# Layer 2 attention scores by 32x64 tiles of the array, one head per row group and PSUM bank; a subtraction moved from VectorE to GpSimd; VectorE's order changed

## The reference

```
# x: [128, 64, 384]; adj: [128, 64, 64], passed as both spatial and edge encoding
q = (x @ Wq.T).reshape(b, n, 12, 32); k, v likewise (v + bv)
scores = einsum('bqhd,bkhd->bhqk', q, k) * 384**-0.5 + (adj + adj)
scores = where(any(scores != 0, -1), scores, -inf)
p = nan_to_num(softmax(scores, -1))
out = einsum('bhqk,bkhd->bqhd', p, v).reshape(b, n, 384) @ Wo.T + bo
x = layernorm(x + out)
```

## Time and profile before

| | us |
|---|---|
| median of 3 runs | 2038.37 (2036.07 to 2038.49) |
| the profiled execution, its own time | 2036.05 |
| its span, first to last instruction | 2034.2 |
| PE busy | 1960.5 (96%) |
| DVE busy | 1389.9 (68%) |
| ACT busy | 1130.7 (56%) |
| POOL busy | 415.3 (20%) |

### The profile page before, as it was taken

One profiled execution on the slowest core, in us unless ns is written; L12 is line 12 of the kernel. 1 busy time (PEld: TensorE's weight loads), 2 busy tenths in 40 slices (PEclk: granted clock), 3 DMA queues, 4 the chain that ended last, 5 costly groups with the idle time before them and its releaser, 6 DMA issues.

```text
span 2034.2 us, 46192 instructions
## 1 busy us (share of the span) xinstructions
PE 1960.5 (96%) x16192; PEld 1881.2 (92%) x16192; DVE 1389.9 (68%) x2622; ACT 1130.7 (56%) x2454; POOL 415.3 (20%) x555
## 2 busy tenths in 40 slices
PE   6599999999999999999999999997999999999997
PEld 5589999999999999999999999987999999999996
DVE  6647767666766767666766767655776776777676
ACT  4346555655566555655566555634555555565565
POOL 3012112121212112121212112121121221222122
PEclk8799999999999999999999999998999999999999
DMA  7524444444444444434444444434322222222221
GB/s 189 147 79 118 105 134 107 123 106 125 114 120 117 107 131 107 125 105 125 114 121 116 109 128 108 116 81 108 86 69 76 83 75 72 81 78 68 81 83 58
DMA packets 268787, 213.52 MB, mean 105 GB/s; under 512 B 142928, under 2 KB 251216, under 8 KB 268752
## 3 DMA queue, kind: packets, MB, share of 16 engines
q1 hardware_dynamic: 268752, 213.06, 39.1%
HBM read 120.34 MB, written 79.69 MB: 98 GB/s over the span
## 4 chain that ended last, share of the span: by engine, by line
PE 93%; DVE 2%; DMA 2%; issue 1%; SPq 1%; ACT 1%; POOL 0%; ACTq 0%; POOLq 0%; DVEq 0%
PE a_bank L406 58%; PE b_bank L1242 15%; PE b_banks L1242 5%; PE b_banks L1284 4%; PE a_bank L477 3%; PE b_bank L1307 2%; PE a_bank L462 2%; PE b_banks L1294 2%; PE b_bank L1317 1%; DMA a_hid_stage<-in_L_gnn_w 1%; SPq L247 1%; DMA a_work<-x_turned 1%; DMA x_turned<-a_work 0%; DMA a_work<-in_L_gnn_wk 0%; DVE xt_lo L793 0%
## 5 line engine op out<-in xcount | busy, mean ns | idle before, releaser
L406 PE MATMUL a_bank<-a_x1t_hi,a_w_hi 128*128 128x256 f32 x1152 | 327.4, 284 | 9.8 <-DVE a_x1t_lo L808 8.3
L406 PE MATMUL a_bank<-a_x1t_hi,a_w_lo 128*128 128x256 f32 x1152 | 323.9, 281 | 0.0
L406 PE MATMUL a_bank<-a_x1t_lo,a_w_hi 128*128 128x256 f32 x1152 | 323.9, 281 | 0.0
L658 ACT ACTIVATE a_work<-a_bank,a_b 128x256 f32<-128x256 f32 x384 | 159.9, 467 | 234.3 <-PE a_bank L406 233.9
L823 DVE TENSOR_TENSOR a_hid_lo<-a_work,a_hid_hi 128x512 fp32r<-128x512 f32 x192 | 130.7, 694 | 192.7 <-ACT a_hid_hi L663 192.7
L406 PE MATMUL a_bank<-a_w_hi,a_hid_hi 128*128 128x384 f32 x768 | 258.2, 336 | 0.0
L406 PE MATMUL a_bank<-a_w_hi,a_hid_lo 128*128 128x384 f32 x768 | 258.2, 336 | 0.0
L406 PE MATMUL a_bank<-a_w_lo,a_hid_hi 128*128 128x384 f32 x768 | 258.0, 336 | 0.0
L406 PEld LDWEIGHTS a_bank<-a_x1t_hi,a_w_hi 128*128 128x128 f32 x1152 | 220.0, 191 | 18.7 <-issue 9.9
L406 PEld LDWEIGHTS a_bank<-a_x1t_lo,a_w_hi 128*128 128x128 f32 x1152 | 220.6, 191 | 0.0
L406 PEld LDWEIGHTS a_bank<-a_x1t_hi,a_w_lo 128*128 128x128 f32 x1152 | 219.4, 190 | 0.0
(11 more groups left out here) (162 smaller groups left out, 5666.4 us busy)
## 6 DMA issues: line engine op xcount, KB each, us to landing
a_work<-in_x SPq DMA_DIRECT2D x64, 384.0 KB, 3.2
p_turned<-a_work SPq DMA_DIRECT2D x256, 64.0 KB, 1.8
a_work<-p_turned SPq DMA_DIRECT2D x32, 512.0 KB, 3.2
xt_raw<-in_xT SPq DMA_DIRECT2D x32, 384.0 KB, 3.9
ctx_turned<-a_work SPq DMA_DIRECT2D x256, 48.0 KB, 1.7
a_work<-ctx_turned SPq DMA_DIRECT2D x32, 384.0 KB, 3.1
x_turned<-a_work SPq DMA_DIRECT2D x256, 48.0 KB, 1.7
a_work<-x_turned SPq DMA_DIRECT2D x32, 384.0 KB, 3.9
```

What stands on the lines that cost most here:

```text
L406: r = pe.matmul(out, lhs[a], rhs[b], start=first and n == 0, stop=last and n == 2)
L658: r = act.activation(silu[:, p % 2, s * GROUP:(s + 1) * GROUP], A[p % 3][:, s * GROUP:(s + 1) * GROUP], ACT.Silu, bias=b1[:, m:m + 1])
```

## The change

Scores are computed with one 32-row tile for each head. Queries and keys go, unmasked, into one buffer `qk_t`, both scaled by the root of 0.5 * SCALE1 on the way out of PSUM, so that their product has the scale already. For each tile t, feature block k, head i of the block and graph s one product takes 32 rows (partitions 32i to 32i + 31) of 64 query columns as weights and streams 64 key columns. Row group i writes PSUM bank i of a four-bank tensor `four`; the old pairs of banks `two[t]` are now views of it. All scores of a group, of both tiles, are one stage with one semaphore increment, and each tile's scores lie in all four banks.

```diff
-            def scores(g, t, back):
-                if t == 0:
-                    pe.wait_ge(q_done, 2 * (g + 1))
-                    pe.wait_ge(k_done, g + 1)
+            def scores(g, back):
+                pe.wait_ge(q_done, 2 * (g + 1))
+                pe.wait_ge(k_done, g + 1)
                 if not back:
                     pe.wait_ge(*free["y2_done"])
                 if back:
-                    pe.wait_ge(pt_done, TILES * (g - 1) + t + 1)
-                for k in range(KT):
-                    b0, b1_, h = SPAN1[k]
-                    for s in range(2):
-                        n = TILES * t + s
-                        r = pe.matmul(two[t][64 * s:64 * s + 64, h * NODES:(h + b1_ - b0) * NODES],
-                                      q[:, k, n * NODES:(n + 1) * NODES],
-                                      k_blocks[:, n, b0:b1_, :].rearrange("p b n -> p (b n)"),
-                                      start=True, stop=True, skip_group_check=True)
+                    pe.wait_ge(pt_done, TILES * g)
+                for t in range(TILES):
+                    for k in range(KT):
+                        for i in range(ROWS):
+                            row = slice(32 * i, 32 * i + 32)
+                            for s in range(2):
+                                nodes = slice((TILES * t + s) * NODES, (TILES * t + s + 1) * NODES)
+                                at = (KT * t + k) * NODES
+                                r = pe.matmul(four[64 * s:64 * s + 64, i, at:at + NODES], qk_t[row, k, nodes],
+                                              qk_t[row, KT + k, nodes], start=True, stop=True, skip_group_check=True)
                 r.then_inc(s_mm, 1)
...
             def attn_out(g, t, front):
                 pe.wait_ge(ctxt_lo, TILES * g + t + 1)
-                if front:
-                    pe.wait_ge(biased, TILES * (g + 1) + t + 1)
+                if front and t == 0:
+                    pe.wait_ge(biased, TILES * (g + 2))
...
             def take_q(g, u):
-                if u == 0:
-                    act.activation(q[:, 0:2, :].rearrange("p k n -> p (k n)"), bank[:], ACT.Copy).then_inc(q_done, 1)
-                    return
-                act.activation(q[:, 2, :], bank[:, 0:GROUP], ACT.Copy)
-                for b in range(*SPAN1[0][:2]):
-                    r = act.activation(k_blocks[:, :, b, :], bank[:, GROUP:2 * GROUP].rearrange("p (g n) -> p g n", g=GB),
-                                       ACT.Copy, scale=mask[:, b:b + 1])
+                act.activation(qk_t[:, 2 * u:2 * u + 2, :].rearrange("p k n -> p (k n)"), one[QK_BANK[u]][:], ACT.Copy,
+                               scale=QK_SCALE).then_inc(q_done, 1)
...
-            def xt_low(g):
-                dve.wait_ge(xt_hi, g + 1)
...
             def take_k(g):
-                for k in (1, 2):
...
+                dve.tensor_scalar(qk_t[:, 4:6, :].rearrange("p k n -> p (k n)"), one[QK_BANK[2]][:], QK_SCALE, None,
+                                  ALU.mult).then_inc(k_done, 1)
...
+            def add_adj(g, t):
+                if t == 0:
+                    dve.wait_ge(s_mm, g + 1)
+                    dve.wait_ge(adj_loaded, 16 * (g + 1))
                 wait(dve, shifted, TILES * (g - 1) + t + 1)
+                dve.tensor_tensor(score[:, t, :].rearrange("p (k i n) -> p k i n", k=KT, i=ROWS),
+                                  four[:, :, S // ROWS * t:S // ROWS * (t + 1)].rearrange("p i (k n) -> p k i n", k=KT),
+                                  adj_in[:, t, :].unsqueeze(1).unsqueeze(1).broadcast_to([P, KT, ROWS, NODES]),
+                                  ALU.add).then_inc(biased, 1)
...
-                if front and more:
-                    xt_low(g + 1)
                 if front:
-                    soften(g, 0)
+                    for t in range(TILES):
+                        add_adj(g, t)
                 if back:
                     for t in range(TILES):
                         ctxt_low(b, t)
                 if front:
-                    soften(g, 1)
+                    for t in range(TILES):
+                        find_max(g, t)
```

More of the change, by code:

```diff
@@ L287, in load_late @@
                     load_row(shared[name], name + "1", late_loaded)
-                for dst, name in ((shared["mask"], "mask1"), (shared["ident"], "ident")):
-                    sp.dma_start(dst[:], w[name]).then_inc(late_loaded, 16)
+                sp.dma_start(shared["ident"][:], w["ident"]).then_inc(late_loaded, 16)
             def load_w1(i):
@@ L1136, in layer1 @@
     S = H1 * NODES
+    ROWS = P // DH1
+    QK_SCALE = (0.5 * SCALE1) ** 0.5
     with ExitStack() as ctx:
@@ L1141, in layer1 @@
         one = [ctx.enter_context(nc.psum_tensor(f"b_bank{i}", [P, 512], F32)) for i in range(4)]
-        two = [ctx.enter_context(nc.psum_tensor(f"b_banks{i}", [P, 1024], F32)) for i in range(2)]
+        four = ctx.enter_context(nc.psum_tensor("b_banks", [P, 4, 512], F32))
+        two = [four[:, 2 * t:2 * t + 2, :].rearrange("p b c -> p (b c)") for t in range(TILES)]
         QK_BANK = (1, 0, 2)
@@ L1342, in step @@
                 if front:
-                    for t in range(TILES):
-                        scores(g, t, back)
+                    scores(g, back)
                 if back:
@@ L1375, in take_q @@
             def take_q(g, u):
-                wait(act, s_mm, TILES * g)
+                wait(act, s_mm, g)
                 act.wait_ge(qk_mm, 3 * g + u + 1)
-                bank = one[QK_BANK[u]]
-                if u == 0:
-                    act.activation(q[:, 0:2, :].rearrange("p k n -> p (k n)"), bank[:], ACT.Copy).then_inc(q_done, 1)
-                    return
-                act.activation(q[:, 2, :], bank[:, 0:GROUP], ACT.Copy)
-                for b in range(*SPAN1[0][:2]):
-                    r = act.activation(k_blocks[:, :, b, :], bank[:, GROUP:2 * GROUP].rearrange("p (g n) -> p g n", g=GB),
-                                       ACT.Copy, scale=mask[:, b:b + 1])
-                r.then_inc(q_done, 1)
+                act.activation(qk_t[:, 2 * u:2 * u + 2, :].rearrange("p k n -> p (k n)"), one[QK_BANK[u]][:], ACT.Copy,
+                               scale=QK_SCALE).then_inc(q_done, 1)
             def keep_v(g, t):
@@ L1465, in _ @@
         def _(dve):
-            def xt_low(g):
-                dve.wait_ge(xt_hi, g + 1)
[L1468 to L1471, removed]
             def take_k(g):
                 dve.wait_ge(qk_mm, 3 * g + 3)
-                wait(dve, s_mm, TILES * g)
-                for k in (1, 2):
[L1477 to L1483, removed]
+                wait(dve, s_mm, g)
+                dve.tensor_scalar(qk_t[:, 4:6, :].rearrange("p k n -> p (k n)"), one[QK_BANK[2]][:], QK_SCALE, None,
+                                  ALU.mult).then_inc(k_done, 1)
             def take_v(g, t):
@@ L1491, in take_v, with find_max @@
                                   bv[:].rearrange("p (h r d) -> p h r d", r=2, d=DH1), ALU.add).then_inc(v_done, 1)
-            def soften(g, t):
-                s = score[:, t, :].rearrange("p (h n) -> p h n", h=H1)
-                dve.wait_ge(s_mm, TILES * g + t + 1)
+            def add_adj(g, t):
                 if t == 0:
+                    dve.wait_ge(s_mm, g + 1)
                     dve.wait_ge(adj_loaded, 16 * (g + 1))
                 wait(dve, shifted, TILES * (g - 1) + t + 1)
-                dve.scalar_tensor_tensor(out=s, in0=two[t][:, 0:S].rearrange("p (h n) -> p h n", h=H1), scalar=0.5 * SCALE1,
-                                         in1=adj_in[:, t, :].unsqueeze(1).broadcast_to([P, H1, NODES]),
-                                         op0=ALU.mult, op1=ALU.add).then_inc(biased, 1)
+                dve.tensor_tensor(score[:, t, :].rearrange("p (k i n) -> p k i n", k=KT, i=ROWS),
+                                  four[:, :, S // ROWS * t:S // ROWS * (t + 1)].rearrange("p i (k n) -> p k i n", k=KT),
+                                  adj_in[:, t, :].unsqueeze(1).unsqueeze(1).broadcast_to([P, KT, ROWS, NODES]),
+                                  ALU.add).then_inc(biased, 1)
+            def find_max(g, t):
                 dve.wait_ge(biased, TILES * g + t + 1)
-                dve.tensor_reduce(smax[:, t, :], s, AX_X, ALU.max).then_inc(maxed, 1)
+                dve.tensor_reduce(smax[:, t, :], score[:, t, :].rearrange("p (h n) -> p h n", h=H1), AX_X, ALU.max).then_inc(
+                    maxed, 1)
             def find_magnitude(g, t):
@@ L1584, in _, with xt_low @@
         def _(pool):
+            def xt_low(g):
+                pool.wait_ge(xt_hi, g + 1)
+                pool.tensor_tensor(xt[1][:].rearrange("p k (n j) -> p k n j", j=32),
+                                  xt_raw.rearrange("p (n k j) -> p k n j", k=KT, j=32),
+                                  xt[0][:].bitcast(F32).rearrange("p k (n j) -> p k n j", j=32),
+                                  ALU.subtract).then_inc(xt_lo, 1)
             def shift(g, t):
@@ L1604, in step @@
```

(2 more changed lines are left out.)

16 lines of the change are left out of this document (8 added, 8 removed).

## The result

The kernel after the change takes 2055.35 us, median of 4 runs (2053.31 to 2059.4); the kernel before, on the same chip, takes 2037.22 (2033.43 to 2038.49). The ratio is 1.0095, 95% interval [1.0071, 1.0118]: slower by 18 us. Forecast was 2021, with a range up to 2048.

The account below looks back on a forecast made before the run. PE was taken to bound 31 of 32 second-layer groups; 30 x (-0.43) = -12.9, group 0 -2.6 and the last group +0.4 gave -15.1 us from 2036.05, forecast 2021, with an 8-in-10 range of 1997 to 2048.

Parts of the forecast that it names:

- x's low part on POOL: Second layer: the subtraction moved from DVE takes 1.47 us on POOL, covered by 2.2 us; 0.95 us freed on DVE.
- Scores and switch: PE's score stage in each group: 2.0 us instead of 2.59, plus 0.16 for an added tile-shape switch, -0.43 us.
- the first rival: Scores: all eight tiles run at once, PE then waits for DVE's ctx; 1987 to 1997 us, chance 0.16.
- The second rival: Scores: never more than two tiles at work, slower than before; 2047 or 2057 us, chance 0.25.
- DVE's order: Both adds before the low parts in steady groups: slack 0.55 us before PE's projection, so the reordering costs nothing.
- Queries and keys: DVE's 2.36 us become one pass of 0.6 us, ACT's four masked copies go; nothing gained in steady groups.
- Group 0: Second layer's first group: scores start 1.7 us earlier and take 4.5 us instead of 5.39; together -2.6 us.
- The last group: Second layer's end: the first add waits for both tiles' scores, so y is late and the group loses 0.4 us.

Follow-up runs that it names:

- low_dve: The changed kernel with x's low part back on DVE behind take_ctx, the rest of the change kept: 2021.42 us, ratio 0.993 to the kernel before.
- one_input: pad, with DVE's reciprocal written to PSUM so its product reads one SBUF and one PSUM operand; x's low part stays on POOL: 1995.69 us, ratio 0.98.
- pad: The changed kernel with an unused tile of 48 bytes a partition where the mask was: 2041.29 us, ratio 1.003 to the kernel before.
- low_pool: The kernel before, with only x's low part moved to the head of POOL's step: 2040.73 us, ratio 1.0027.
- two_tiles: pad_low_dve, with the row group as outermost loop of the scores, so only two tiles can be at work at a time: 2030.18 us, ratio 0.9968.
- old_order: one_input, with DVE's order of before in the scores' part: 2038.0 us, ratio 1.001 to the kernel before.
- moved_mask: The kernel before, with the mask's tile behind the first layer's tiles and nothing else changed: 2045.91 us, ratio 1.0048.
- pad_low_dve: The changed kernel with both the unused 48-byte tile and x's low part back on DVE: 2014.85 us, ratio 0.9893 to the kernel before.

## Why the prediction was wrong

**The step that failed** is "x's low part on POOL". I priced the subtraction by its own duration, called it covered by 2.2 us, and counted the 0.95 us freed on DVE as more cover. PE indeed never waits for `xt_lo` in the changed kernel. What I left out is what the instruction does to the others while it runs: it lies exactly over `take_ctx`, the DVE work on which PE depends next. low_dve and one_input show it: 1.47 us a group, 45.6 us in all between pad and one_input; low_pool shows the same collision where PE is busy and little waits. The size of the subtraction was off too, 1.82 us and not 1.47.

The trace of the kernel before already held such a pair, in the first layer. `a_work - a_smax`, two SBUF operands, takes 0.69 us alone, and over 1.4 us in 28 of its 64 instances, beside POOL's bias add; DVE, then POOL:

```profile
809.17 1.46 DVE L840 TENSOR_TENSOR a_work<-a_work,a_smax 128x512 f32<-128x512 f32 x1
...
811.99 0.69 DVE L840 TENSOR_TENSOR a_work<-a_work,a_smax 128x512 f32<-128x512 f32 x1
```

```profile
809.04 1.04 POOL L1055 TENSOR_TENSOR a_work<-a_work,a_bo 128x384 f32<-128x384 f32 x1
```

**Two errors of opposite sign.** Without the collision and with the old placement the change wins 40 us (one_input), not the 15 of the sum, and its 1995.69 lies just below the range, which began at 1997. So the gain was put too low, and the two costs at nothing.

**Scores and switch.** Sized at 2.0 us, measured 1.2: the first rival, which had 0.16, was the right one. That handing over the instructions holds the pace near 21 ns was wrong: the mean is 12.5 ns, and in a burst of eight they start 6 to 7 ns apart (two_tiles above). Its wait also came as I had put it, the transposes for DVE's ctx; one_input, 17.64 us a group and 1995.69 us, lies in that rival's range (1987 to 1997). The second rival's pace is the one that two_tiles shows, 2.43 us, just at the point I had named as deciding. It failed as a forecast because the loop puts neighbours on different tiles and banks. The added switch of tile shape, 0.16 us in the sum, does not show: pv's piece is 1.57 us instead of 1.56, and the transposes behind the 32x64 tiles take 0.81 us in two_tiles, as before. Their 0.93 in one_input comes with a wait: DVE's ctx of the second tile, which the fourth transpose needs, ends only at 1527.75.

**DVE's order**, costed at nothing, was right in that the new order leaves no wait. I did not see that the new layout needs it: without it 1.3 us a group (old_order).

**Queries and keys**: right; 0.69 us for DVE's pass, no wait in steady groups.

**The first layer** was taken as unchanged. It is 8.7 us longer by placement (pad, moved_mask). I had no row for it, and the diff's one line on the mask tile was read as memory freed.

**Group 0**: the scores start 2.1 us behind the memset instead of 3.8, the 1.7 us earlier that I had forecast, and fell from 5.39 to 1.76 us at the same clock of 0.50, better than my 4.5. But PE then waits for DVE: the two passes of L913, 0.86 us before, take 2.36 beside POOL's subtraction (1.87 us there), so PE starts qk at 1434.55, 7.45 us behind the memset, and needs 9.14 us for 54 matmuls. No gain of 2.6 us was left; without POOL's subtraction beside it (pad_low_dve) group 0, from its first values matmul to the next group's, takes 24.58 us instead of 25.80, a gain of 1.2.

**The last group** was forecast at +0.4 and measured at -0.8: PE's scores end so much earlier that both adds start earlier.

**The clock**: I had no term for it. The new wait of 1.3 us in each group is followed, in three of 30 groups, by a granted clock on the 1.2 GHz level for some 3.4 us, 1.5 us each. With the unused tile it is one group, and in steady groups none in the kernels in which PE does not wait for `take_ctx`. A wait alone does not do it: in old_order PE waits 1.1 us for DVE's second add in every group (31.5 us in 30), and the clock stays up. What brings it down in three groups stays open.

## What to carry to other kernels

When an instruction moves to POOL, look not only at who waits for its result, but at each DVE instruction that will run beside it: one with two SBUF operands is held until POOL's ends, however small it is, and in group 0 one with an SBUF tensor and two SBUF scalars was too; one operand in PSUM avoided it here without any other change. The trace before the change may show such pairs already: look for an instruction with two durations. Small matmuls on distinct tiles of the array overlap as far as the order of the loops lets neighbours fall on different tiles (and, here, banks). And when a change adds or removes an SBUF tile, compare the parts that it does not touch: a dummy tile tells placement from the change itself.

## What the runs showed of the hardware that I had not expected

- A 12-element DVE product took 1.64 us beside a POOL instruction, and 0.17 with one operand in PSUM. A DVE `tensor_scalar` with one SBUF tensor and two SBUF scalars took 1.97 us beside it, and 0.475 alone.
- 96 matmuls of 32x64 tiles took about 1.2 us (12.5 ns each) in an order that spreads them over eight tiles and four banks, and 2.43 us (25.3 ns) over two tiles and one bank at a time. At the 1.2 GHz level they took 1.76 us (18.3 ns).
- A shift of SBUF tiles by 64 bytes, down or up, changed the feed-forward f32r matmuls of the first layer from 284 to 286 ns mean, and its steady group from 41.57 to 41.83 us, some 8 us of 1420. 128 bytes up gave 286 ns there too, but 2 ns less in the query, key and value matmuls, and 41.69 us.
- POOL took 1.82 us to subtract 768 elements into an fp32r tile in a permuted order, and 1.47 for the same number in `shift`.
